# Layer 0's feed-forward as one block worked in pieces, rows loaded in four parts, and the output stored from inside the last stage

## What is computed

```python
def _fp8_matmul(x2d, w):
    scale_x = jnp.maximum(jnp.max(jnp.abs(x2d)) / FP8_MAX, 1e-06)
    scale_w = jnp.maximum(jnp.max(jnp.abs(w)) / FP8_MAX, 1e-06)
    x8 = (x2d / scale_x).astype(jnp.float8_e4m3fn)
    w8 = (w / scale_w).astype(jnp.float8_e4m3fn)
    out = jnp.matmul(x8.astype(x2d.dtype), w8.astype(x2d.dtype).T)
    return out * (scale_x * scale_w)
...
h = _fp8_matmul(x2d, w_fc)
h = jnp.square(jax.nn.relu(h))
out = _fp8_matmul(h, w_proj)
...
x = x + _L0_xattn_ref(_layernorm(x, axis=-1), ctx_2048, ctx_2048, ...)
x = x + _L0_ffn_ref(_layernorm(x, axis=-1), L0_ffn_w_fc, L0_ffn_w_proj)
...
x = x + _L3_ffn_ref(_layernorm(x, axis=-1), L3_ffn_wg, L3_ffn_w1, L3_ffn_v1, L3_ffn_w2)
```

## Time and profile before

| what | us |
|---|---|
| median of three runs (2937.6 to 2942.43) | 2940.05 |
| the profiled execution | 2937.88 |
| its span, from first to last instruction | 2936.1 |
| PE busy in it, share | 2291.1, 78% |
| DVE busy, share | 1847.2, 63% |
| ACT busy, share | 1493.4, 51% |
| POOL busy, share | 1495.4, 51% |
| mean granted TensorE clock, of 1 | 0.897 |

### The profile page before, as it was taken

The page is one execution under the profiler, slowest core; times in us unless marked ns, Lnnn a source line. Parts: engine busy times, 40 slices in busy tenths (PEclk is TensorE's granted clock), DMA queues, the critical chain, the costliest instruction groups (busy, mean ns, idle before and its releaser), DMA issues. The chain is left out here.

```text
span 2936.1 us, 46383 instructions
## 1 busy us (share of the span) xinstructions
PE 2291.1 (78%) x14566; PEld 1674.8 (57%) x14574; DVE 1847.2 (63%) x3739; ACT 1493.4 (51%) x3353; POOL 1495.4 (51%) x1487
## 2 busy tenths in 40 slices
PE   4788233685897667679739999976999996999997
PEld 2333012344654433268527777764888884788885
DVE  3777378564545535345557888865888875666565
ACT  0667252573120026534348888864888874344443
POOL 5442000631000144158337888863888883788882
PEclk9999665796999769979869999997999997899999
DMA  5232100443021223323220000001000000334343
GB/s 126 66 86 69 52 0 7 141 146 124 34 113 65 52 58 87 76 79 97 67 87 1 0 0 0 0 30 54 6 5 5 4 1 18 89 113 114 101 113 92
DMA packets 119750, 174.63 MB, mean 59 GB/s; under 512 B 25389, under 2 KB 79693, under 8 KB 116383
## 3 DMA queue, kind: packets, MB, share of 16 engines
q1 hardware_dynamic: 119583, 172.53, 20.7%
HBM read 122.49 MB, written 11.48 MB: 46 GB/s over the span
## 5 line engine op out<-in xcount | busy, mean ns | idle before, releaser
L478 DVE TENSOR_REDUCE a_mraw<-a_first_ps 128x4 f32<-128x1024 f32 (+1 forms) x256 | 310.4, 1221 | 148.6 <-PE a_first_ps L329 148.2
L386 ACT ACTIVATE a_et<-a_second_ps 128x1024 f32<-128x1024 f32 x256 | 262.1, 1024 | 160.4 <-PE a_second_ps L347 158.3
L2819 POOL TENSOR_SCALAR a3o_raw<-a3o_raw,a3o_mu,a3o_dev 128x128 f32<-128x128 f32 x320 | 304.6, 964 | 4.8 <-issue 4.8
L2819 POOL TENSOR_SCALAR a3x_raw<-a3x_raw,a3x_mu,a3x_dev 128x128 f32<-128x128 f32 x320 | 283.6, 899 | 4.8 <-issue 4.8
L1669 DVE TENSOR_TENSOR f3e_hidden_low<-f3e_hidden,f3e_hidden_high 128x512 fp32r<-128x512 f32 x96 | 115.9, 1207 | 126.3 <-ACT f3e_hidden_high L1627 125.9
L1538 POOL TENSOR_TENSOR f3e_product<-f3e_silu,f3e_up 128x512 f32<-128x512 f32 x96 | 143.4, 1496 | 73.2 <-PE f3e_u_ps L1554 46.0
L364 PE MATMUL a_o_ps<-a_et,a_vt 128*32 128x256 f32 x2048 | 167.5, 399 | 7.4 <-ACT a_osb L416 6.2
L347 PE MATMUL a_second_ps<-a_qs,a_ks 64*128 64x256 bf16 (+2 forms) x896 | 117.6, 298 | 65.2 <-ACT a_et L386 55.7
L329 PE MATMUL a_first_ps<-a_ks,a_qs 64*128 64x256 bf16 (+2 forms) x1280 | 123.1, 267 | 19.1 <-DMA a_ks<-a_parts 10.3
L347 PEld LDWEIGHTS a_second_ps<-a_qs,a_ks 64*128 64x128 bf16 (+1 forms) x896 | 42.0, 96 | 165.1 <-ACT a_et L386 129.5
L1620 ACT ACTIVATE f3e_silu<-f3e_g_ps 128x512 f32<-128x512 f32 x96 | 57.4, 598 | 144.3 <-PE f3e_g_ps L1554 137.3
(11 more groups left out here) (547 smaller groups left out, 6829.9 us busy)
## 6 DMA issues: line engine op xcount, KB each, us to landing
f_w<-in_f_w SPq DMA_DIRECT2D x16, 1216.0 KB, 8.6
a_qs<-a_parts SPq DMA_DIRECT2D x144, 128.0 KB, 2.4
f_raw<-in_f_w SPq DMA_DIRECT2D x60, 256.0 KB, 3.3
a_ks<-a_parts SPq DMA_DIRECT2D x96, 128.0 KB, 2.4
f3e_spread<-f3e_shares SPq DMA_DIRECT2D x64, 192.0 KB, 3.0
f2e_spread<-f2e_shares SPq DMA_DIRECT2D x36, 256.0 KB, 3.4
f3e_spread<-f3e_shares SPq DMA_DIRECT2D x64, 128.0 KB, 3.0
f_raw<-in_f_w SPq DMA_DIRECT2D x60, 128.0 KB, 3.3
```

What stands on the lines that cost most here:

```text
L386: self.nc.scalar.activation(self.et[:, g % self.WAVES_HELD, :, :], self.second_ps[:, :, :], ACT.Exp, scale=self.scale).then_inc(self.e_rea ...
L478: v.tensor_reduce(out, self.first_ps[:, g % 2, :, :].rearrange("p u (c n) -> p u c n", n=N), AX.X, ALU.max).then_inc(self.max_taken, 1)
L2819: mm = nc.gpsimd.tensor_scalar(head, head, mu[:, h:h + 1], dev[:, h:h + 1], ALU.subtract, ALU.mult)
```

## The change

- The one DMA that loads X becomes four of four batches each, with a semaphore each and no wait; the statistics of the first stage wait for each part as they come to it (`arrived`).
- Layer 0's feed-forward becomes one block with one set of semaphores. Loops are written out. GpSimd normalises every fourth row, VectorE the other twelve. Weights and rows are rounded in eight pieces of 1024 columns: two of wfc, four of the rows, two of wproj.
- `round_fp8` has three passes on VectorE. ScalarE now makes two copies of a piece: one scaled, and one scaled and multiplied by 2^20 into `power`. VectorE makes the magic number of `power` in one pass by two bit operations. It adds and subtracts the larger of that and a constant.
- The up projection goes by 512 rows: transposes of four batches, one copy, and four chunks of four matmuls of 512 columns. Each has a Relu and a peak of 1024 columns. The pieces of wproj are rounded after all this.
- The down projection goes by one batch. Four squares come ahead of the loop, the others inside it, three batches ahead.
- In the last stage X's first half is stored by eight DMAs on SyncE's queue between the loads of the second half's steps 6 to 13; the second half after the last `add`, four DMAs from SyncE and four from ScalarE. The storing block at the end is gone.

```diff
-                with dve.Fori(0, B // 8) as i:
...
+                for k, piece_in in enumerate(arrived):
+                    dve.wait_ge(piece_in, 16)
+                    for b in range(k * B // len(arrived), (k + 1) * B // len(arrived)):
+                        nc.vector.bn_stats(stats[:, b, :], X[:, b, :]).then_inc(stats_done, 1)
...
+            def store(engine, h, g, stored):
+
+                j, k = g % 4, g // 4
+                engine.dma_start(out.rearrange("b p n -> p b n")[16 * g:16 * g + 16, 8 * h:8 * h + 8, :],
+                                 X[2 * j + k:P:8, 8 * h:8 * h + 8, :]).then_inc(stored, 16)
...
+                        if out is not None and 0 <= n - H - 6 < 8:
+                            sp.wait_ge(added, 2)
+                            store(sp, 0, n - H - 6, stored_early)
+                    if out is not None:
+                        sp.wait_ge(added, 4)
+                        for g in range(4):
+                            store(sp, 1, g, stored_sp)
+                        sp.wait_ge(stored_early, 8 * 16)
+                        sp.wait_ge(stored_sp, 4 * 16)
...
+                    if out is not None:
+                        act.wait_ge(added, 4)
+                        for g in range(4, 8):
+                            store(act, 1, g, stored_act)
+                        act.wait_ge(stored_act, 4 * 16)
...
+def round_fp8(nc, v, m, out):
+
+
+    low = 1.5 * 2.0 ** 14
+    nc.vector.tensor_scalar(m.bitcast(I32), m.bitcast(I32), EXPONENT_BITS, HALF_BIT, ALU.bitwise_and, ALU.bitwise_or)
     nc.vector.drain()
-    nc.vector.tensor_scalar(magic, magic, 2.0 ** -6, 1.5 * 2.0 ** 20, ALU.max, ALU.mult)
+    nc.vector.scalar_tensor_tensor(v, m, low, v, ALU.max, ALU.add)
     nc.vector.drain()
...
+    return nc.vector.scalar_tensor_tensor(out, m, low, v, ALU.max, ALU.subtract)
...
+                for b in range(3, B, 4):
+                    nc.gpsimd.tensor_scalar(xn[:, b, :], X[:, b, :], mean[:, b:b + 1], rstd[:, b:b + 1],
+                                            ALU.subtract, ALU.mult).then_inc(row_there, 1)
...
+                for n in FC + ROWS:
+                    round_piece(n)
+                for n in range(B):
+                    tb, j = divmod(n, 4)
+                    dve.wait_ge(h_taken, n + 1)
+                    v.tensor_reduce(peaks[:, n:n + 1], hid[:, 2 * j:2 * j + 2, tb * 512:tb * 512 + 512], AX.XY,
+                                    ALU.max).then_inc(h_peak, 1)
+                dve.wait_ge(h_peak, B)
+                v.tensor_reduce(peak[:, 0:1], peaks[:, :], AX.X, ALU.max).then_inc(hid_peak_ready, 1)
+                round_piece(PROJ[0])
...
+                round_piece(PROJ[1])
...
+                for b in range(B):
+                    dve.wait_ge(hid_scaled, b + 1)
+                    wait(dve, y_done, b - 1)
+                    round_fp8(nc, hidden(b), power_of_hidden(b), hid8[:, b % 2, :, :]).then_inc(hid_ready, 1)
+                    if b:
+                        add(b - 1)
+                add(B - 1)
...
+                def scale_piece(n):
+                    wait(act, rounded, n - 1)
+                    values, out, k = piece(n)
+                    nc.scalar.activation(power_of(n), values, ACT.Identity, scale=raised[:, k:k + 1])
+                    nc.scalar.activation(values, values, ACT.Identity, scale=unscale[:, k:k + 1]).then_inc(scaled, 1)
...
+                for n in PROJ:
+                    scale_piece(n)
+                for b in range(4):
+                    square(b)
+                act.wait_ge(hid_unscale_ready, 1)
+                for b in range(B):
+                    if b >= 1 and b + 3 < B:
+                        square(b + 3)
+                    act.wait_ge(squared, b + 1)
+                    if b < 2:
+                        act.wait_ge(rounded, len(FC + ROWS + PROJ))
+                    else:
+                        act.wait_ge(hid_ready, b - 1)
+                    nc.scalar.activation(power_of_hidden(b), hidden(b), ACT.Identity, scale=raised[:, 3:4])
+                    nc.scalar.activation(hidden(b), hidden(b), ACT.Identity, scale=unscale[:, 3:4]).then_inc(hid_scaled, 1)
...
+                for tb in range(4):
+                    pe.wait_ge(rounded, ROWS[tb] + 1)
+                    wait(pe, taken, tb)
...
+                    pe.wait_ge(taken, tb + 1)
+                    for j in range(4):
+                        n = 4 * tb + j
+                        wait(pe, h_taken, n - 1)
...
-                sp.dma_start(X[:, :, :], dram["x"]).then_inc(x_in, 16)
-                sp.wait_ge(x_in, 16)
...
+                for k in range(4):
+                    sp.dma_start(X[:, 4 * k:4 * k + 4, :], dram["x"][:, 4 * k:4 * k + 4, :]).then_inc(x_in[k], 16)
```

More of the change, by code:

```diff
@@ L1783, in stage_l0_ffn @@
     OC = HID // P
+    FC, ROWS, PROJ = (0, 1), (2, 3, 4, 5), (6, 7)
     with Stage(nc, "f0") as st:
[L1785 to L1793 removed]
@@ L1857, in _ @@
                         for u in range(2):
[L1859 to L1860 removed]
+                            oc = 2 * j + u
                             for c in range(2):
[L1862 to L1864 removed]
@@ L1866, in _ @@
-                @block.scalar
-                def _(act):
-                    act.wait_ge(unscale_ready, 1)
-                    xf = xn[:, :, :].rearrange("p b n -> p (b n)")
-                    for src, k in ((xf[:, 0:2048], 0), (xf[:, 2048:], 0), (wfc[:, :], 1), (wproj[:, :], 2)):
-                        nc.scalar.activation(src, src, ACT.Identity, scale=unscale[:, k:k + 1]).then_inc(scaled, 1)
-                    with act.Fori(0, B // 2) as i:
-                        for u in range(2):
-                            act.wait_ge(turned, i * 2 + (u + 1))
-                            nc.scalar.copy(x8t[:, :, bass.ds((i * 2 + u) * P, P)], tp[:, u, 0:2, :]).then_inc(taken, 1)
@@ new lines, in _ @@
+                                last = nc.tensor.matmul(h_ps[:, n % 2, u, :], wfc8[:, c, oc * P:oc * P + P],
+                                                        x8t[:, c, tb * 512:tb * 512 + 512],
+                                                        start=(c == 0), stop=(c == 1))
+                        last.then_inc(h_done, 1)
+                for b in range(B):
+                    pe.wait_ge(hid_ready, b + 1)
+                    wait(pe, y_added, b - 1)
+                    for oc in range(OC):
+                        last = nc.tensor.matmul(y_ps[:, b % 2, 0:D], hid8[:, b % 2, oc, :], wproj8[:, oc, :],
+                                                start=(oc == 0), stop=(oc == OC - 1))
+                    last.then_inc(y_done, 1)
```

420 lines of the change are left out of this document (192 added, 228 removed).

## The result

The changed kernel takes **2901.24 us** (median of 4 runs, 2900.51 to 2902.20), the kernel before beside it 2938.82 (2937.13 to 2942.43): a ratio of 0.9871, 95% interval 0.9854 to 0.9888, so 37.6 us faster (by the interval 33 to 43), where 35.4 was forecast; in absolute time 2904.7 was forecast. The profiled execution took 2901.81, its span is 2900.0 against 2936.1.

| stretch | before | after | won | forecast |
|---|---|---|---|---|
| span's start to TensorE's first matmul | 20.04 | 15.51 | 4.53 | 4.3 |
| rest of layer 0's attention | 314.90 | 315.82 | -0.92 | 0 |
| layer 0's feed-forward | 165.48 | 138.63 | 26.85 | 25.8 |
| layer 1 to X's last addition | 2420.58 | 2420.38 | 0.20 | 0 |
| last addition to the end | 15.10 | 9.66 | 5.44 | 5.3 |

The account below looks back on a forecast made before the run. Layer 0's feed-forward was taken as a chain through VectorE, with no engine computing at the span's start and end. Gains of 4.3 + 25.8 + 5.3 = 35.4 us gave 2904.7 against 2940.05; range 2897 to 2910, 2896 to 2915 with half clock.

Parts of the forecast that it names:

- The start: Span's start, X loaded in four parts: statistics end at 10.8 instead of 15.1, 4.3 us less.
- Up to the first scaling: Layer 0's feed-forward, rows and peaks before ScalarE's first scaling: ScalarE starts at 357.0, 10.4 us less.
- A rounding: Three VectorE passes on 1024 columns, 0.70 + 1.22 + 1.22 + about 0.2: 3.34 us a piece.
- Up projection: Layer 0's feed-forward, rounds of 512 rows at 6.05 us: last peak at 400.0 against 425.0, 25.0 us less.
- Given back: Between last peak and down loop, both wproj pieces on the path: loop starts at 410.6 instead of 430.27, 19.7 us less.
- The loop: Down projection, 16 x 3.34 + 15 x 0.42 = 59.7 us; last addition ends at 472.8 instead of 498.76.
- The stage's end: Behind the feed-forward's last addition: one block less but 27 clears in place of nine, 0.2 us more.
- The stage as a whole: Layer 0's feed-forward, all its gains and losses together: 25.8 us less.
- The end: From X's last addition to span's end: 5.3 us less with DMA engines as the limit, 7.7 if issue-bound.
- clock at 1.00 in the three rounds: Rival for the up projection: TensorE stays at half clock, 9.2 us more, 2914; chance 12%.
- bit pass at 0.685: Rival for the roundings: the two-operation bit pass runs at one element a cycle, 12.5 us more, 2917; chance 6%.
- the slower rival: Two-tensor passes in the feed-forward's roundings stretch, needing GpSimd at work beside VectorE; at the row's ratio 2983; chance 2%.

## Why the prediction was right, point by point

- **The start**, 4.3: 4.53. The constants behind X's four parts cost nothing to speak of: the last statistic ends at 10.60, where 10.8 was forecast. About 1 us was lost again in the attention, where the forecast had nothing.
- **Up to the first scaling**, 10.4: 9.3. The step that failed is "twelve rows written out cost what a statistic of the same width does, 0.33: 4.0 us". The row was the right one, and without GpSimd it is 0.33; but GpSimd's rows were set beside VectorE's at no cost, and they stretched them to 0.42, 1.0 us in all. The same paragraph took 0.74 for a row of the old loop; that is what it cost in this build, and 0.52 in two others. Had it been 0.52 in this build, 3.5 of the 9.3 would not have been there to win.
- **A rounding**, 3.34 a piece: 3.20. The passes came out within 0.015 (0.685, 1.225, 1.225). What was mis-sized is the gaps: 0.07 behind the first and the second pass, and the next instruction starts 0.08 before the end of the third, 0.06 in all instead of 0.2. Both unknown forms went at the values taken and not at their upper ends.
- **Up projection**, last peak 25.0 earlier: 23.7. Of the 1.3 the start of the scaling is 1.1, nearly all of it the rows. Faster roundings (6 x 0.14 = 0.8) and slower rounds (3 x 0.35 = 1.1) nearly cancel. In a round the Relus are what was mis-sized: from the first to what follows the fourth it is 4.26 and not 3.92. From one start to the next it is 1.01, 1.23, 1.01 and 1.01.
- **Given back**: from the last peak's end to the loop 10.6 in the forecast, 10.2 measured, in the order foretold, with ScalarE's wait for the last rounding (1.60) as its last link.
- **The loop**: 59.7 for sixteen steps, 57.1 measured; with the last product and the last addition 62.2 and 59.3. VectorE bounds it: one more pass lengthens every step by its length, and twelve squares do not.
- **The stage's end**, +0.2: +1.2. The forecast named 27 clears in place of nine and one block less, but it gave the difference 0.2 without a row. SyncE's 27 clears take 2.0 us (467.37 to 469.35), 0.06 each and a pause of 0.4. Eight of before's nine took 0.44, and the ninth stood in the block that is gone, worth some 0.35. Nothing covers the clears.
- **The stage as a whole**: 25.8 forecast, 26.85 measured. That it is so near is in part luck. 1.3 less at the last peak and 1.0 less at the stage's end stand against 0.4 more behind the peak and 2.9 more in the loop, and 2.2 of those 2.9 come from gaps that were priced too high. By the kernel with four passes, the pass saved is 16.3 of the 26.85, and the rows are 6.8 (11.76 less 4.97), of which 3.5 hang on this build of before. How the rest divides between one block, smaller pieces and moved work was not taken apart.
- **The end**, 5.3: 5.44. The DMA engines were the limit, not SyncE's issue: in the change they are busy 94% from 2892 to 2894 and 96% from 2894 to 2896, and one queue instead of two costs 0.4 us. The Trainium skill (DMA: Bandwidth & Descriptors, "Issuing engines are not separate DMA queues") says that issuing from several engines saves only the time of issuing, and the trace agrees.
- **The rivals**: clock at 1.00 in the three rounds, bit pass at 0.685, start and end both won, no pass beyond 1.23. The one contention in the stage is where the slower rival said that it would have to be, with GpSimd at work, but it lasts 5 us. No other stage changed by more than executions differ, if the attention's 0.92 is counted so.

## What to carry to other kernels

Price a pass by the row of its kind at another width, and then ask of each such price what else works at that time: the rows of this sum were right per instruction and wrong in what stood beside them. Give gaps a row too: 0.14 us too much beside each rounding made the loop's term 2.2 too long. Clears of semaphores between stages are path, here 0.06 us each and a pause of 0.4. After a stage has been rebuilt, look for the last wait in front of its longest loop; here three small moves of ScalarE's and VectorE's order, all read off one stretch of 12 us, gave 5.4 us more in the stage.

## What the runs showed of the hardware that was not expected

- The step of a short loop on VectorE, one instruction of 0.41 us, is 0.75 or 0.52 us by where its code stands: eight drains far ahead of it are enough. A comparison of two kernels can carry 3.5 us of that in a stage that neither touches.
- A tensor_scalar of VectorE with one tensor input and 256 columns goes from 0.407 us to 0.474 in the median and 0.639 at most beside GpSimd's tensor_scalar, which itself takes 1.31 where another stage has 1.22.
- TensorE's granted clock in one and the same program was 1.00 in one execution and 0.91 in another over the same 40 us, with 0.7 us more in a stage of 315 us; in another program it was 0.91 and 0.83, with 1.7 more.
- A run of semaphore clears on SyncE has a pause of 0.4 us at a fixed place of SyncE's code: with two instructions fewer ahead, it comes two clears later.
